# Hybrid layer: order of four engines' work around the second norm and the short filter in the mixer

## The chip, the cores and the metric

One core of one Trainium2 chip runs the whole program. The metric is the device time of one launch in microseconds (us), the median of several runs. The engines of the core are TensorE (PE; its weight loads are a row of their own, PEld), VectorE (DVE), ScalarE (ACT), GpSimd (POOL) and SyncE (SP), which issues most DMAs.

## The reference

The input x has 8 sequences of 2048 tokens with 256 channels. Four residual layers follow each other, each on a layer norm of x:

```
x = x + scan_mixer(norm(x))       # in_proj, selective scan over 8 heads, rmsnorm, out_proj
x = x + gated_ffn(norm(x))        # shift mix, sigmoid(r) * (relu(k)**2 @ W_v)
x = x + long_conv(norm(x))        # in_w, short filter of 3 taps, long convolution, out_w
x = x + gated_ffn(norm(x))
...
h = alpha * h + beta * Bx_prev + gamma * Bx_t     # one step of the scan, state 64 x 128 per head
y_t = einsum("bhpn,bhn->bhp", h, C_t)
```

The keys B and C of the scan are rotated by an angle that accumulates over the tokens. The short filter is a causal convolution of 3 taps on each of 768 channels.

## The kernel before, in words

The program has five stages one behind the other. Two short ones normalise the tokens and work out the scan's parameters and the filter's taps. The third, `mixer_and_first_ffn`, is the longest; it runs from about 240 us to about 3500 us. The fourth is the long convolution, the fifth the projection and the second gated layer. The change touches the third alone.

**Tiles and quads.** A tile is 128 tokens, so there are 128 tiles; four consecutive tiles are a quad, so there are 32 quads. The scan, the rotation and the output projection work on one tile at a time. The gated layer, the second norm and the first product of the third layer (`widen`) work on a whole quad.

**Rounds.** The body of every engine is written out by hand. `rounds(body)` runs 34 rounds; each has four places q = 0 to 3. In a place, `tile(q, lag, step)` issues a step for the tile that is `lag` tiles behind the current one, and `quad(lag, step)` issues a step for the quad that is `lag` rounds behind. An engine executes its steps strictly in the written order. Steps of different engines are tied by one semaphore per kind of step: `wait_for(engine, step, i)` waits until step number i is done.

**The steps of a tile.** TensorE makes the products of C and B for two groups of four heads (`project_bc`, L721), VectorE rotates them into two halves (`rotate`, L1159 and L1160), GpSimd adds the halves (`add_turned`, L1059), TensorE turns the sum over (`turn_over`, L744) and ScalarE copies it out of the bank (`copy_turned`, L924). GpSimd makes `masked_steps` (L1050), TensorE sums them to the decay's logs (`decay_logs`, L729 and L730), ScalarE takes their exponentials (`exponentials`, L908) and the bounds of the diagonal (`own_bounds`, L915), VectorE cuts the one by the other (`cut_decay`, L1173). One tile later TensorE makes the product `gram` (L754), VectorE weighs it with the decay (`weigh_gram`, L1179), TensorE forms the `outputs` (L769, L772), and VectorE takes them (`take_y`, L1187 and L1189). `new_state` (L780), `fade_state` (L1071) and `carry_state` (L1194) hand the state on. `decay_values` (L1065) and `gate_values` (L1167) weigh the values. A tile later still the squares are made (`square_y`, L929), paired (`pair_sums`, L1077) and summed (`sum_over`, L787), and the result is projected (`project_out`, L793) and added to x (`residual1`, L1212).

**The steps of a quad that the change moves or passes.** `residual2` (L1237, with the statistics at L1199, L1202 and L1205) adds the gated layer to x, in two halves. `layer_rstd` (L1091 to L1094) makes scale and shift on GpSimd, `normalised` (L940) the normalised tokens on ScalarE, both in two halves. `x2n_over` (L833) turns them over on TensorE; it waits for both halves. `x2_hi` (L969) and `x2_lo` (L1243) split the turned values into two parts, and six times `widen` (L840) multiplies them with the weights, one block of 128 channels at a time. `take_up` (L979, L980) takes a block out of the bank with the first tap, `taps` (L1248) adds the other two taps out of the same bank, and `before_filter` (L1110 to L1118) makes the two columns that reach over the quad's edge.

**Banks.** The eight banks of PSUM are shared by fixed rotas. All gram products and the values share one bank: the second `gram` of a tile waits for the first `weigh_gram`. The logs and the new state share another: the second `decay_logs` of a tile waits for `carry_state`. Two banks carry everything behind the scan, in the order of `BANK_POST`; in bank 1 `sum_over` of q = 2 comes after the fifth `widen` (numbered from 0) and therefore waits for `taps` 5, and the second half of `x2n_over` comes after the output projection of q = 0 and waits for `residual1`.

```
BANK_GRAM = (("gram0", "mix0", 1, -1), ("gram1", "mix1", 1, -1), ("values", "gate_values", 1, 0))
BANK_ARG = (("logs0", "exp0", 1, 0), ("new_state", "carry_state", 1, -1), ("logs1", "exp1", 1, 0))
Y_BANK, OUT_BANK, W_BANK = (1, 0, 1, 1), (1, 0, 1, 1), (1, 0, 1, 1, 0, 1)
```

Of the kernel before, what the change touches and what calls it, by code (L numbers as in the profile page):

```python
# [524 lines left out]
def mixer_and_first_ffn(nc, ctx, t):  # L525
# [116 lines left out]
    with nc.Block() as block:  # L642
# [69 lines left out]
        def _(pe):  # L712
# [131 lines left out]
            def body(tile, quad, n):  # L844
                for q in range(QUAD):
                    tile(q, 0, project_bc, 0, 1)
                    tile(q, 0, project_bc, 0, 0)
                    if q == 2:
                        quad(2, widen, 5)
# [35 lines left out]
                    if q == 0:  # L885
                        quad(2, x2n_over)
# [4 lines left out]
                    tile(q, 0, decay_logs, 1)  # L891
            rounds(body)

        @block.scalar
        def _(act):
# [88 lines left out]
            def body(tile, quad, n):  # L984
                for q in range(QUAD):
                    tile(q, -1, split_xnT)
                    tile(q, 1, exponentials, 1)
                    tile(q, 2, square_y)
                    tile(q, 0, own_bounds, 0)
                    if q == 1:  # L990
                        quad(2, x2_hi, 0)
                        quad(2, x2_hi, 1)
                    if q == 2:
                        quad(2, take_up, 5)
                    if q == 3:
                        quad(1, tanh, 0)
                    tile(q, 1, copy_turned, 1, 1)
                    tile(q, 1, copy_turned, 1, 0)
                    tile(q, 2, mean_square, q)
                    if q == 0:  # L1000
                        quad(2, normalised, 2, 0)
                    if q == 1:
                        quad(2, take_up, 0)
                    if q == 2:
                        quad(1, earlier_token, 0)
                        quad(1, earlier_token, 1)
                    if q == 3:
                        quad(1, tanh, 1)
                    tile(q, 0, exponentials, 0)
                    tile(q, 0, own_bounds, 1)  # L1010
                    if q == 0:
                        quad(2, normalised, 2, 1)
                    if q == 1:
                        quad(2, take_up, 1)
                        quad(2, take_up, 2)
                    tile(q, 0, copy_turned, 0, 1)
                    if q == 1:
                        quad(2, take_up, 3)
                    if q == 2:
                        quad(1, relu_squared, 0)  # L1020
                    tile(q, 0, copy_turned, 0, 0)
                    if q == 1:
                        quad(1, normalised, 1, 0)
                        quad(1, normalised, 1, 1)
                        quad(2, take_up, 4)
                    if q == 2:
                        quad(1, relu_squared, 1)
# [3 lines left out]
        def _(pool):  # L1031
# [90 lines left out]
            def body(tile, quad, n):  # L1122
                for q in range(QUAD):
# [6 lines left out]
                    tile(q, 1, fade_state)  # L1130
                    if q == 0:
                        quad(2, layer_rstd, 2, 0)
                        quad(2, before_filter)
                    tile(q, 2, scan_rstd)
                    tile(q, 0, add_turned, 1, 1)
                    tile(q, 0, masked_steps, 1)
                    if q == 0:
                        quad(2, layer_rstd, 2, 1)
                    tile(q, 0, add_turned, 1, 0)
# [8 lines left out]
        def _(dve):  # L1148
# [114 lines left out]
            def body(tile, quad, n):  # L1263
                for q in range(QUAD):
                    tile(q, 0, rotate, 0, 1)
                    tile(q, 1, cut_decay, 1)
                    tile(q, 0, rotate, 0, 0)
                    if q == 0:
                        quad(2, residual2, 0)
# [3 lines left out]
                    if q == 2:  # L1273
                        quad(2, taps, 4)
                    tile(q, 1, weigh_gram, 0)
                    if q == 2:
                        quad(2, taps, 5)
                    tile(q, 0, rotate, 1, 1)
                    tile(q, 1, weigh_gram, 1)
                    if q == 0:  # L1280
                        quad(2, residual2, 1)
# [10 lines left out]
                    tile(q, 0, rotate, 1, 0)  # L1292
                    if q == 1:
# [564 lines left out]
```

How the kernel before makes its waits and increments, by code:

```python
def wait(eng, sem, value):  # L34
    if isinstance(value, int) and value <= 0:
        return
    eng.wait_ge(sem, value)
# [47 lines left out]
        @block.sync  # L86
        def _(sp):
            sp.wait_ge(consts, 1)
            sp.dma_start(w_scal[:, :, 0:24], t["w_scal"].rearrange("(k p) n -> p k n", p=128)).then_inc(w_in, 16)
            def load(n, g, v):
                wait(sp, xn_ready, n - R + 1)
                sp.dma_start(xg[v % R][:, :, :], t["x"][bass.ds(n * 4 * TOK, 4 * TOK), :]
                             .rearrange("(q p) c -> p q c", p=128)).then_inc(x_in[v % R], 16)
            rounds(sp, lambda on: on(0, load))
# [74 lines left out]
        @block.tensor  # L170
        def _(pe):
            pe.wait_ge(consts, 2)
            pe.wait_ge(w_in, 16)
            def transpose(n, g, v):
# [31 lines left out]
        @block.scalar  # L207
# [13 lines left out]
                p = v % 2  # L221
                wait(act, rows_ready, n + 1)
                wait(act, scal_ready, n - 1)
                nc.scalar.copy(scT[p][:, :], p_scT[p][:, :]).then_inc(rows_taken, 1)
            def body(on):
                on(1, copy_and_store)
                on(2, take_rows)
            rounds(act, body)
            for p in range(2):
                act.wait_ge(xt_out[p], 16 * GROUPS // 2)
# [40 lines left out]
        @block.sync  # L272
# [16 lines left out]
            for k in range(KT):  # L289
                sp.dma_start(taps[:, k, TOK - 1:], t["decay"][k * 128:(k + 1) * 128, :]).then_inc(s["weights_in"], 16)
            sp.wait_ge(s["scan_dve"], PARAMS)
            sp.dma_start(t["params_dram"], params[:, :, :]).then_inc(s["stored"], 16)
```

## Time and profile before

| what | value |
|---|---|
| median of 3 runs | 4691.2 us (4690.49 to 4694.54) |
| the profiled execution | 4688.05 us |
| its span | 4686.3 us |
| TensorE busy | 4287.6 us (91%) |
| VectorE busy | 3240.8 us (69%) |
| GpSimd busy | 2370.2 us (51%) |
| ScalarE busy | 2158.3 us (46%) |
| mean granted clock of TensorE | 0.959 |

A time of "start, length" is counted from the start of the span. Consecutive operations of one engine overlap a little in the records, so the distance of two starts is often some 0.1 us less than the length shown. "idle before" is the time in which the engine had nothing to run just before an instruction, and the name behind the arrow is what the records show as ending it; "issue" means that the profile shows nothing for it, although the engine may have stood at a semaphore. The granted clock is a share of TensorE's full clock: 1.00 stands for 2.4 GHz, 0.50 for 1.2 GHz.

### The profile page before, as it was taken

To read this page: it belongs to the slowest core of one execution; us is meant where nothing else is said; L and a number is where in the kernel's file an instruction comes from. 1 tells how busy PE (TensorE), PEld (TensorE's weight loads), DVE (VectorE), ACT (ScalarE), POOL (GpSimd) and SP (SyncE) were. 2 spreads that over 40 slices of the span, in tenths; PEclk is the share of its full clock that TensorE was granted. 3 is DMA by queue.
4 is the path that set the end of the run, shared out by engine and by line. 5 is a ranking of instruction groups with operands and counts; after the bars stand their busy time and mean duration, and the time that the engine had idled before them with its cause. 6 is when DMAs were issued, how large, how long until landed. Compare 5 with 4: busy or idle time off the path is not lost. (4 is left out here: it accounts for less than half of the span.)

```text
span 4686.3 us, 118726 instructions
## 1 busy us (share of the span) xinstructions
PE 4287.6 (91%) x39924; PEld 3567.5 (76%) x39924; DVE 3240.8 (69%) x6737; ACT 2158.3 (46%) x5046; POOL 2370.2 (51%) x3284
## 2 busy tenths in 40 slices
PE   5399999999999999999999999999959999989999
PEld 3177777777777777777777777777738888878888
DVE  8766666666677666667666676666645666658888
ACT  3244444444444444444444444444426666645555
POOL 3275666665666665666565666565610000016666
PEclk9699999999999999999999999999979999999999
DMA  8311111111111111111111111111127666633333
GB/s 274 134 50 36 35 37 42 40 37 43 37 37 46 36 37 46 34 37 48 36 35 46 34 38 48 35 37 43 32 53 191 183 183 181 183 110 106 105 105 95
DMA packets 369775, 347.50 MB, mean 74 GB/s; under 512 B 24954, under 2 KB 343290, under 8 KB 360186
## 3 DMA queue, kind: packets, MB, share of 16 engines
q1 hardware_dynamic: 352380, 323.98, 23.3%
q10 hardware_dynamic: 16896, 16.78, 1.1%
q8 instruction: 324, 5.31, 0.5%
q14 instruction: 175, 1.43, 0.1%
HBM read 232.01 MB, written 108.66 MB: 73 GB/s over the span
## 5 line engine op out<-in xcount | busy, mean ns | idle before, releaser
L721 PE MATMUL bank<-w_bc,xnT 128*128 128x512 f32 x3072 | 814.7, 408 | 10.7 <-POOL xnT L1042 10.7
L924 ACT COPY turned_t<-bank 128x512 f32<-128x512 f32 x512 | 299.9, 586 | 857.5 <-PE bank L744 857.4
L721 PEld LDWEIGHTS bank<-w_bc,xnT 128*128 128x128 f32 x3072 | 569.5, 192 | 149.9 <-issue 35.3
L1050 POOL TENSOR_TENSOR steps<-upto,par 128x512 fp32r<-128x512 f32 x512 | 551.0, 1097 | 6.2 <-PE bank L730 6.2
L1455 PE MATMUL p_yc<-sig,toep 64*64 64x256 f32 (+14 forms) x16384 | 539.6, 282 | 15.2 <-issue 11.9
L1455 PEld LDWEIGHTS p_yc<-sig,toep 64*64 64x64 f32 x16384 | 476.0, 132 | 91.0 <-issue 44.5
L1159 DVE TENSOR_TENSOR rot<-bank,par 128x512 f32<-128x512 f32 x512 | 350.0, 684 | 247.1 <-PE bank L721 165.5
L1059 POOL TENSOR_TENSOR turned_b<-rot 128x512 f32<-128x512 f32 x256 | 325.3, 1271 | 306.5 <-DVE rot L1160 306.1
L754 PEld LDWEIGHTS bank<-turned_t 128*128 128x128 f32 x2048 | 300.7, 214 | 127.8 <-issue 105.3
L754 PE MATMUL bank<-turned_t 128*128 128x128 f32 x2048 | 309.5, 300 | 93.9 <-issue 92.3
L1179 DVE TENSOR_TENSOR mix<-bank,decay 128x512 f32<-128x512 f32 x256 | 175.6, 686 | 298.5 <-PE bank L754 297.9
L1042 POOL TENSOR_TENSOR xnT<-xnT_raw,xnT 128x256 fp32r<-128x256 f32 x128 | 94.8, 741 | 504.0 <-ACT xnT L903 504.0
L1604 POOL MEMSET xT<- 128x258 f32 x1 | 0.3, 314 | 686.7 <-POOLq L1349 686.7
L1160 DVE TENSOR_TENSOR rot<-bank,par 128x512 f32<-128x512 f32 x512 | 347.1, 678 | 0.0
L840 PE MATMUL bank<-x2T,in_w 128*128 128x512 f32 x1152 | 315.8, 411 | 26.6 <-ACT ms_eps L934 17.0
L1059 POOL TENSOR_TENSOR turned_c<-rot 128x512 f32<-128x512 f32 x256 | 332.4, 1299 | 1.9 <-DVE rot L1160 1.8
L915 ACT ACTIVATE own<-bound,par 128x128 f32<-128x128 f32 x1024 | 326.4, 399 | 0.4 <-DMA par<-params_dram 0.4
L1248 DVE SCALAR_TENSOR_TENSOR conv<-bank,short,conv 128x511 f32<-128x511 f32 (+1 forms) x384 | 286.1, 745 | 47.6 <-ACT conv L980 30.9
L840 PEld LDWEIGHTS bank<-x2T,in_w 128*128 128x128 f32 x1152 | 215.0, 191 | 77.8 <-DVE x2T L1243 20.4
L1487 DVE TENSOR_TENSOR ys<-p_yc,odd_y 64x256 f32<-64x256 f32 x256 | 95.6, 411 | 238.7 <-ACT odd_y L1406 238.7
L780 PEld LDWEIGHTS bank<-u_w,turned_b 128*128 128x128 f32 x2048 | 250.5, 193 | 10.8 <-issue 0.3
L940 ACT ACTIVATE xn<-x_quad,shift,rstd 128x256 f32<-128x256 f32 x256 | 136.5, 593 | 264.2 <-POOL shift L1094 264.2
(264 smaller groups left out, 9727.3 us busy)
## 6 DMA issues: line engine op xcount, KB each, us to landing
toep<-taps_dram SPq DMA_DIRECT2D x256, 260.0 KB, 4.2
el<-el_dram SPq DMA_DIRECT2D x256, 128.0 KB, 3.1
xg<-arg_x SPq DMA_DIRECT2D x32, 512.0 KB, 4.9
xnT_dram<-xt_g ACTq DMA_DIRECT2D x32, 512.0 KB, 4.2
xnT_raw<-xnT_dram SPq DMA_DIRECT2D x128, 128.0 KB, 2.5
x_quad<-arg_x SPq DMA_DIRECT2D x32, 512.0 KB, 3.9
x_dram<-x_quad SPq DMA_DIRECT2D x32, 512.0 KB, 3.8
x0T_dram<-conv SPq DMA_DIRECT2D x32, 512.0 KB, 2.8
```

The lines of the kernel that those rows point to most:

```text
L721: last = mm(p_bc[c][:, :], xnT[w.q % 2][p][:, k, :], w_bc[q][:, k, c * 1024 + g * W4:c * 1024 + (g + 1) * W4], start=(n == 0), stop=(n == ...
L754: last = mm(p_gram[:, c], turned_t[g][0][:, c], turned_t[g][1][:, c], start=True, stop=True)
L780: last = mm(p_state[:, v], turned(w, h // GROUP, 0)[:, (h % GROUP) * STATE:(h % GROUP + 1) * STATE], u_w[:, v], start=True, stop=True)
L840: last = mm(p_post[W_BANK[e]][:, :], in_w[q][:, k, e * 128:(e + 1) * 128], x2T[p][:, k, :], start=(m == 0), stop=(m == len(SPLIT) - 1))
L915: last = s_.activation(own[g][:, h * TOK:(h + 1) * TOK], bound[:, :], ACT.Identity, scale=par[w.p][:, w.q, P_RHO + g * GROUP + h:P_RHO + g ...
L924: s_.copy(turned_t[g][c][:, :], p_tr[:, :]).then_inc(s[f"copy_{BC[c]}"], 1)
L1050: last = g_.tensor_tensor(heads(steps[p][:, :]), upto[:, :].unsqueeze(1).broadcast_to([128, GROUP, TOK]), over(of_group(P_A + p * HEADS, w ...
L1059: g_.tensor_tensor(turned(w, g, c)[:, :], rot1[c][:, :], rot2[c][:, :], ALU.add).then_inc(s[f"turn_{BC[c]}"], 1)
L1159: v_.tensor_tensor(heads(rot1[c][:, :]), heads(p_bc[c][:, :]), cos, ALU.mult)
L1160: v_.tensor_tensor(parts(rot2[c][:, :]), parts(p_bc[c][:, :])[:, :, ::-1, :], over(sin.rearrange("p (h s) -> p h s", s=2), STATE // 2), AL ...
L1248: last = v_.scalar_tensor_tensor(out=conv[:, e, back:], in0=p_post[W_BANK[e]][:, 0:SPAN - back], scalar=short[:, e, 2 - back:3 - back], in ...
L1455: last = mm(by_seq(p_y[p][c][odd * H:(odd + 1) * H, 0:2 * TILES])[:, :, first:], toep[n % SLOTS][c * H:(c + 1) * H, lag * H:(lag + 1) * H] ...
```

## The change

Steps change their places within the body of four engines; none is added, removed or altered.

- TensorE: `widen` 5 leaves q = 2 for the end of q = 1; in q = 0 `x2n_over` comes behind the second `decay_logs` instead of ahead of it.
- ScalarE: in q = 1 and 2 `x2_hi` and `take_up` 5 come ahead of `square_y` and the first `own_bounds`; in q = 0 the two halves of `normalised` each come behind a `copy_turned` (the first was ahead of the exponentials).
- GpSimd, q = 0: the second `masked_steps` comes ahead of the `add_turned` of group 1; the halves of `layer_rstd` come behind one `add_turned` each, and `before_filter` behind all.
- VectorE: in q = 0 the halves of `residual2` come behind the second weighing and behind the last rotation, where they were ahead of the first weighing and behind the second; in q = 1 `x2_lo` comes ahead of `cut_decay` and the second rotation; in q = 2 `taps` 4 comes ahead of the first rotation and `taps` 5 behind it.

```diff
@@ tensor @@
-                    if q == 2:
-                        quad(2, widen, 5)
                     if q == 3:
                         quad(1, receptance, 0)
                     tile(q, 1, gram, 0)
...
                     tile(q, 0, project_u)
-                    if q == 0:
-                        quad(2, x2n_over)
                     if q == 1:
                         quad(2, widen, 4)
                     if q == 2:
                         quad(1, key, 1)
                     tile(q, 0, decay_logs, 1)
+                    if q == 0:
+                        quad(2, x2n_over)
+                    if q == 1:
+                        quad(2, widen, 5)
@@ scalar @@
                     tile(q, 1, exponentials, 1)
-                    tile(q, 2, square_y)
-                    tile(q, 0, own_bounds, 0)
                     if q == 1:
                         quad(2, x2_hi, 0)
                         quad(2, x2_hi, 1)
                     if q == 2:
                         quad(2, take_up, 5)
+                    tile(q, 2, square_y)
+                    tile(q, 0, own_bounds, 0)
...
                     tile(q, 2, mean_square, q)
-                    if q == 0:
-                        quad(2, normalised, 2, 0)
...
                     tile(q, 0, own_bounds, 1)
-                    if q == 0:
-                        quad(2, normalised, 2, 1)
...
                     tile(q, 0, copy_turned, 0, 1)
+                    if q == 0:
+                        quad(2, normalised, 2, 0)
...
                     tile(q, 0, copy_turned, 0, 0)
+                    if q == 0:
+                        quad(2, normalised, 2, 1)
@@ gpsimd @@
                     tile(q, 1, fade_state)
+                    tile(q, 2, scan_rstd)
+                    tile(q, 0, masked_steps, 1)
+                    tile(q, 0, add_turned, 1, 1)
                     if q == 0:
                         quad(2, layer_rstd, 2, 0)
-                        quad(2, before_filter)
-                    tile(q, 2, scan_rstd)
-                    tile(q, 0, add_turned, 1, 1)
-                    tile(q, 0, masked_steps, 1)
+                    tile(q, 0, add_turned, 1, 0)
                     if q == 0:
                         quad(2, layer_rstd, 2, 1)
-                    tile(q, 0, add_turned, 1, 0)
+                        quad(2, before_filter)
@@ vector @@
+                    if q == 2:
+                        quad(2, taps, 4)
                     tile(q, 0, rotate, 0, 1)
-                    tile(q, 1, cut_decay, 1)
-                    tile(q, 0, rotate, 0, 0)
-                    if q == 0:
-                        quad(2, residual2, 0)
                     if q == 1:
                         quad(2, x2_lo, 0)
                         quad(2, x2_lo, 1)
                     if q == 2:
-                        quad(2, taps, 4)
+                        quad(2, taps, 5)
+                    tile(q, 1, cut_decay, 1)
+                    tile(q, 0, rotate, 0, 0)
                     tile(q, 1, weigh_gram, 0)
-                    if q == 2:
-                        quad(2, taps, 5)
                     tile(q, 0, rotate, 1, 1)
                     tile(q, 1, weigh_gram, 1)
                     if q == 0:
-                        quad(2, residual2, 1)
+                        quad(2, residual2, 0)
...
                     tile(q, 0, rotate, 1, 0)
+                    if q == 0:
+                        quad(2, residual2, 1)
```

## Rows read from the trace of the kernel before

**Rows 1.** The page: shares of the span, and the granted clock in 40 slices.
```profile
PE 4287.6 (91%) x39924; PEld 3567.5 (76%) x39924; DVE 3240.8 (69%) x6737; ACT 2158.3 (46%) x5046; POOL 2370.2 (51%) x3284
...
PEclk9699999999999999999999999999979999999999
```

**Rows 2.** Windows: busy time per engine (PE, PEld, DVE, ACT, POOL), then granted clock.
```profile
500.00:3100.00 2600.00, 2450.05 (x15261) 2030.93 (x15261) 1782.34 (x3161) 1139.18 (x2649) 1603.13 (x1971) 0.97 0.13 40
...
1602.00:1608.00 6.00, 5.73 (x28) 4.86 (x29) 4.15 (x10) 2.74 (x7) 5.43 (x14) 0.50 0.01 4
...
1550.00:1554.00 4.00, 2.76 (x20) 2.43 (x20) 1.28 (x3) 2.13 (x7) 4.00 (x5) 1.00 0.00 0
...
1652.00:1656.00 4.00, 3.80 (x17) 3.41 (x18) 0.00 (x0) 3.38 (x10) 3.60 (x5) 0.57 0.02 4
```

**Rows 3.** Waits of PE from 500 to 3100 us: total, times, longest.
```profile
PE bank L754 <- issue: 76.9, 25, 3.3
PE bank L787 <- DVE conv L1248: 41.8, 26, 1.9
PE bank L840 <- ACT ms_eps L934: 14.5, 26, 0.7
```

**Rows 4.** Timeline of PE in one q = 0: start, length, line, shapes, count.
```profile
1594.97 1.06 PE L754 MATMUL bank<-turned_t 128*128 128x128 f32 x8
1595.86 0.60 PE L744 MATMUL bank<-ident,turned_c 128*128 128x128 f32 x4
...
1602.27 2.04 PE L754 MATMUL bank<-turned_t 128*128 128x128 f32 x8 [3.28 <-issue]
...
1615.48 1.03 PE L833 MATMUL bank<-ident,xn 128*128 128x128 f32 x8
1616.27 0.47 PE L729 MATMUL bank<-steps,after_r 128*128 128x512 f32 x1
...
1616.81 0.39 PE L721 MATMUL bank<-w_bc,xnT 128*128 128x512 f32 x1
```

**Rows 5.** Timeline of DVE in the same q = 0.
```profile
1595.04 1.43 DVE L1173 TENSOR_TENSOR decay<-decay,own 128x512 f32<-128x512 f32 x1
...
1597.84 1.31 DVE L1237 SCALAR_TENSOR_TENSOR x_quad<-gate,x_quad 128x512 f32<-128x512 f32 x1 [0.17 <-issue]
...
1601.21 0.68 DVE L1179 TENSOR_TENSOR mix<-bank,decay 128x512 f32<-128x512 f32 x1
1601.81 0.67 DVE L1159 TENSOR_TENSOR rot<-bank,par 128x512 f32<-128x512 f32 x1
...
1605.20 0.69 DVE L1237 SCALAR_TENSOR_TENSOR x_quad<-gate,x_quad 128x512 f32<-128x512 f32 x1 [0.16 <-issue]
...
1607.97 0.41 DVE L1187 TENSOR_TENSOR y_from<-bank,el 128x256 f32<-128x256 f32 x1
...
1608.82 0.69 DVE L1159 TENSOR_TENSOR rot<-bank,par 128x512 f32<-128x512 f32 x1
...
1614.93 0.68 DVE L1173 TENSOR_TENSOR decay<-decay,own 128x512 f32<-128x512 f32 x1
```

**Rows 6.** Timelines of three engines around the change from q = 1 to q = 2.
```profile
1541.34 0.77 ACT L980 ACTIVATE conv<-bank,all_taps_b,short 128x512 f32<-128x512 f32 x1
...
1548.53 1.56 DVE L1248 SCALAR_TENSOR_TENSOR conv<-bank,short,conv 128x511 f32<-128x511 f32 x2
...
1550.83 0.35 PE L787 MATMUL bank<-ones,y_sum 128*128 128x1 f32 x2 [1.90 <-DVE conv L1248]
```

**Rows 7.** Timelines of POOL and ACT in the q = 0 of rows 4.
```profile
1597.34 1.27 POOL L1059 TENSOR_TENSOR turned_c<-rot 128x512 f32<-128x512 f32 x1
...
1608.99 0.70 POOL L1091 TENSOR_TENSOR rstd<-var_eps,minus_half 128x2 f32<-128x2 f32 x1
...
1610.00 0.20 POOL L1094 TENSOR_TENSOR shift<-minus_mean,rstd 128x2 f32<-128x2 f32 x1
...
1610.23 1.09 ACT L940 ACTIVATE xn<-x_quad,shift,rstd 128x256 f32<-128x256 f32 x2 [4.00 <-POOL shift L1094]
```

## The prediction

> **What bounds the kernel now.** I read four views in this order: shares and clock slices of the page, the waits of PE over 26 steady rounds of the mixer, one round's engines in order of time, and the windows of granted clock. PE is busy 91% of the span, and its clock is below full in only a few slices [rows 1]. In the mixer, from 500 to 3100 us, PE works 2450 of 2600 us at a mean granted clock of 0.97 [rows 2]. So PE is the bound there, and what can be won is its idle time and the work that it does at half clock.
>
> The idle time has three places that come back in every round of four tiles [rows 3]: the second gram product (L754), 76.9 us in 25 waits, 3.08 each; the sum over the squares (L787), 41.8 us in 26 waits, 1.61 each; the first widening product (L840), 14.5 us in 26, 0.56 each. Together 5.25 us a round. The clock adds its own loss: 3% of 2600 us at half the full rate are 0.03 x 2 x 2600 = 156 us at half clock, which lose 78 us of work, 3.0 us a round. So 8.25 us a round is the ceiling for anything that only reorders, and a round is some 100 us.
>
> The first place is q = 0. PE ends the first decay logs at 1602.27 - 3.28 = 1598.99 and stands for 3.28 us [rows 4]. What it waits for is the gram bank, freed by the weighing (L1179), which runs at 1601.21 to 1601.89 because the first residual2 block stands ahead of it from 1597.84 [rows 5]. After the wait the window 1602 to 1608 has a granted clock of 0.50 [rows 2], the lower of the two levels, 1.2 GHz, and L754 x8 takes 2.04 us where it took 1.06 before the wait [rows 4]. The second place is q = 2: PE stands 1.90 us at L787 until the last taps (L1248, from 1548.53) have read the bank [rows 6]. In a later round of the same kind the clock falls there too: 0.57 over 1652 to 1656 [rows 2].
>
> **The change part by part.** No instruction is added or removed; each one is moved within its own engine's order. No DMA is moved. SP's waits stay (the store of x2 waits for residual2, as before), so its queue is passed by nothing.
>
> *Residual2 behind the weighing (VectorE, q = 0).* The block costs 1601.21 - 1597.84 = 3.37 us in the first place and 1607.97 - 1605.20 = 2.77 in the second [rows 5]; I take 3.1, and keep both ends. It now follows the second weighing, and its other half follows the last rotation. I go through this round again in the new order, with its own durations. Rotations and cut decay end at about 1597.84 - 0.17 = 1597.67, as before. The first weighing starts at once and takes 0.60 start to start (1601.21 to 1601.81) [rows 5]: done at 1598.3, 0.7 us before PE reaches gram 1 at 1598.99. That wait is gone, by this sum, with a margin of 0.7 us. The rotation of group 1 must wait for GpSimd's turned copy, 1597.34 + 1.27 = 1598.6 [rows 7], and takes 1.2 (two operations at 0.60 start to start): to 1599.9. Gram 1 takes 0.89 (1594.97 to 1595.86) [rows 4] and ends at 1599.9, the second weighing at 1600.6. Then residual2 0 (0.17 of drain and 3.1): 1603.9. take_y 0 takes 1608.82 - 1607.97 = 0.85 [rows 5]: 1604.8. Rotation of group 1, other side, 1.2: 1606.0. residual2 1 with its drain, 3.3: 1609.3. GpSimd's rstd to shift takes 1610.00 + 0.20 - 1608.99 = 1.2 [rows 7], ScalarE's norm 1.09 [rows 7]; with some 0.1 us at each handover x2n_over can start at 1612.0.
>
> *Turned copies ahead of the norm (ScalarE) and masked steps behind the first logs (GpSimd).* The exponentials of group 0 no longer wait behind a norm, and GpSimd's second masked steps come before add_turned and the rstd. They fill time in which both engines waited; I cost them at nothing. Their cover is the 4 us that ScalarE waited for the shift before each norm [rows 7]. If it is gone, the delay of the norm falls straight on PE, as below.
>
> *x2n_over behind the second logs (PE, q = 0).* From gram 1 (1602.27) to the next tile (1616.81) PE needs 14.54 us, of which some 5.8 at half clock count half: 11.6 at full clock, 0.79 of it x2n_over (1615.48 to 1616.27) [rows 4]. Unhindered PE would reach x2n_over at 1598.99 + 10.8 = 1609.8. It is not let in before 1612.0. So **2.2 us of waiting come back** where 3.28 went: about 0.5 ahead of the second logs, which need carry_state and with it the end of residual2 1 on VectorE, the rest ahead of x2n_over. Bounds from the two lengths of the block: 1.6 to 2.8 us. Whether the clock falls in the new waits no row can say. From below: not at all, 0. From above: as much as now, 3.0 us a round. The nearest rows are those behind the q = 2 wait (clock at 1.00 over 1550 to 1554 in the one round, 0.57 over 1652 to 1656 in the other) [rows 2], so I take a part of it, 0.85 us a round, half a stretch such as 1652 to 1656 in every round.
>
> *Filter's fifth widening and taps (PE, VectorE, q = 1 and 2).* The fifth product leaves q = 2 and comes at the end of q = 1: the same work on PE. Its taps are then run behind the first rotation instead of behind the weighing, about 5 us before the sum over the squares instead of 1.9 us after it was due, so all 1.61 goes. Taps 4 now stand ahead of the first rotation: their input is taken up by 1541.34 + 0.77 = 1542.1 [rows 6], they end near 1543.7, and the rotation, whose products end 1.4 us later than before, was due near 1544.4. Margin 0.7 us. Cost nothing.
>
> *x2_lo ahead of cut_decay and a rotation (VectorE, q = 1).* The first widening waits for it 0.56 us now. x2_lo ends by the new order before PE is due at widen 0: 0.56 gained. The weighing behind it is late by the same 1.3 us, which still ends about 1 us before gram 1.
>
> **Sum.** Now lost: 3.08 + 1.61 + 0.56 + 3.0 = 8.25 us a round. Left: 2.2 + 0.85 = 3.05. Gain 5.2 us in each of 31 rounds (of 34, those in which all three lags have a quad): 161 us. The profiled execution took 4688.05 us (span 4686.3), 3.1 below the median of 4691.2. 4688 - 161 = 4527, against the median 4530.
>
> **A rule against the change.** The cut decay that runs beside GpSimd's masked steps took 1.43 us, and without them 0.68 [rows 5]. The Trainium skill, "SBUF — State Buffer", "Who interferes with whom", says that a DVE instruction with two SBUF inputs and a GpSimd instruction that reads SBUF exclude each other for a whole instruction, and that order of issue decides who waits. This trace agrees, by the two lengths just named. As a mechanism here: the first operation of each residual2 block has both inputs in SBUF, and the new places put it beside the masked steps and the added turned copies. Each could wait out one more GpSimd operation of 1.0 to 1.3 us, which makes the rival "port" below.
>
> **The rivals.**
> - *The clock falls as before.* The new waits stand close together, 2.2 us within some 3, and the old 3.28 dropped the clock in each round. For: the q = 2 wait of under 2 us did so at times. Against: at times it did not. Left 2.2 + 3.0: gain 3.05 x 31 = 95, time 4596. Chance 0.22.
> - *Port.* Both blocks 1 us longer, wait 4.2, clock lost as before: left 7.2, gain 1.05 x 31 = 33, time 4658. Against: the lengths that I took already hold one such collision (3.37). Chance 0.07.
> - *Better.* The norm is in time to within 1.2 us and the clock stays up: gain 7.05 x 31 = 219, time 4472. Chance 0.09.
> - *Slower.* x2n_over stands in PE's queue ahead of the next tile's products, and x2_lo in VectorE's ahead of the next rotation and the weighing. Every us by which the second norm is late beyond the reckoned 1612.0 is then lost whole. With the clock as before it costs more than the change gains once the wait passes 8.25 - 3.0 = 5.25 us, that is 3 us later than reckoned. Two us more for each block would give a wait of 6.2: 0.95 x 31 = 29 us more, 4720. For: the chain residual2 1, rstd, norm, turn has no slack at all in the new order. Against: its operations have lengths known to 0.6 us. Chance 0.04.
> - *No effect.* The weighing was not what PE waited for, or VectorE becomes the bound over the whole round. VectorE is busy 1782 of 2600 us [rows 2], so only a stretch of it can bind. Time 4690. Chance 0.03.
>
> **How the numbers follow.** My forecast (both waits gone, 2.2 back, clock lost in part) has the remaining 0.55 and reaches from 4485 to 4565. With the clock rival the range is 4482 to 4602, which leaves out the port, the slower case, no effect and part of the better one. A measurement of this kernel can tell about 0.2% (9 us) from no change. Faster by more than that: 0.55 + 0.22 + 0.07 + 0.08, 0.92 in all; within it 0.03; slower 0.05.
>
> **What would show it.** In the changed profile: no wait at L754 with the half clock behind it; L787's wait at L1248 gone; a new wait of PE, 1.5 to 2 us, at L833 for ScalarE's norm, and a short one at L729 or L730; the round near 95 us; clock about 0.99 over the mixer. I am wrong if L754 still waits, if the wait at L833 is over 3 us, or if the granted clock of the mixer is still 0.97.

## The result and the profile after

The changed kernel takes 4491.7 us (median of 4 runs, 4485.8 to 4495.2) against 4690.8 for the kernel before; the ratio is 0.9575, with a 95% interval from 0.9563 to 0.9587. That is 199 us less where 161 were forecast. The profiled execution took 4485.8 us, its span is 4484.1. The number of instructions is the same.

The page of the changed kernel, shares of the span and the granted clock in 40 slices, as in [rows 1]:

```profile
PE 4197.9 (94%) x39924; PEld 3488.0 (78%) x39924; DVE 3222.6 (72%) x6737; ACT 2157.4 (48%) x5046; POOL 2376.0 (53%) x3284
...
PEclk9699999999999999999999999999979999999999
```

PE's busy time fell by 90 us although it does the same work. The clock accounts for it: a mean of 0.959 over 4686.3 us lacks 192 us of full clock, one of 0.978 over 4484.1 us lacks 99, which is 93 less. The window of the mixer shows the same (time, then busy time of PE, PEld, DVE, ACT, POOL, then the granted clock), as in [rows 2]:

```profile
500.00:2900.00 2400.00, 2345.81 (x15012) 1937.76 (x15012) 1745.14 (x3116) 1122.91 (x2613) 1584.99 (x1934) 1.00 0.13 42
```

The clock is 1.00 where it was 0.97: in this stretch it never stands at half, where before it did so for 143 us. PE works 2346 of 2400 us. The waits of PE in the same stretch (total, times, longest), as in [rows 3]:

```profile
PE bank L833 <- ACT xn L940: 20.8, 25, 0.9
PE bank L801 <- issue: 20.0, 52, 0.6
PE bank L840 <- issue: 6.7, 26, 0.4
PE bank L833 <- issue: 2.0, 9, 0.3
```

The waits at L754 and L787 are gone. New is 0.83 us at L833, the turn of the second norm. L801, the turn of the first norm, takes 0.77 us a round in two parts. The stores of x2, one a round, start at 408.0 us first and 3267.7 last, 2859.7 / 31 = 92.2 us apart in the mean; before it was (3466.1 - 412.1) / 31 = 98.5. The last two distances are short ones at the end of the stage (84.4 and 51.1 us now). A full round takes 94.0 us, and took 100.4 (the table in the next section).

One q = 0 on PE, to be held against [rows 4] (start, length, line, shapes, count, idle time before):

```profile
1520.03 0.39 PE L730 MATMUL bank<-steps,after_r 128*128 128x512 f32 x1
1520.40 1.16 PE L754 MATMUL bank<-turned_t 128*128 128x128 f32 x8
...
1531.15 0.40 PE L730 MATMUL bank<-steps,after_r 128*128 128x512 f32 x1
1532.38 1.37 PE L833 MATMUL bank<-ident,xn 128*128 128x128 f32 x8 [0.83 <-ACT xn L940]
1533.50 3.03 PE L721 MATMUL bank<-w_bc,xnT 128*128 128x512 f32 x12
```

Gram 1 follows the logs at once and runs at full clock, 1.16 us instead of 2.04. The same stretch on VectorE, against [rows 5]:

```profile
1519.03 0.68 DVE L1179 TENSOR_TENSOR mix<-bank,decay 128x512 f32<-128x512 f32 x1
...
1522.45 1.37 DVE L1237 SCALAR_TENSOR_TENSOR x_quad<-gate,x_quad 128x512 f32<-128x512 f32 x1 [0.17 <-issue]
...
1525.05 0.22 DVE L1205 TENSOR_SCALAR var_eps<-mean_var 128x2 f32<-128x2 f32 x1
1525.25 0.42 DVE L1187 TENSOR_TENSOR y_from<-bank,el 128x256 f32<-128x256 f32 x1
...
1527.53 0.69 DVE L1237 SCALAR_TENSOR_TENSOR x_quad<-gate,x_quad 128x512 f32<-128x512 f32 x1 [0.16 <-issue]
...
1529.45 0.45 DVE L1205 TENSOR_SCALAR var_eps<-mean_var 128x2 f32<-128x2 f32 x1
1529.81 0.68 DVE L1194 TENSOR_TENSOR state<-bank,state 128x512 f32<-128x512 f32 x1
```

The weighing ends at 1519.71, 0.7 us before gram 1 starts. The two blocks of residual2 take 1525.25 - 1522.45 = 2.80 and 1529.81 - 1527.53 = 2.28 us.

### The profile page after: what moved, and what is told of

The parts are those of the page before. It is cut to its first block and busy times, and to the rows that moved or that the text cites. A ratio compares the mean times of both kernels' runs of the same rounds, so it can differ in the third digit from the quotient of the medians.

```text
span 4484.1 us, 118726 instructions
## 1 busy us (share of the span) xinstructions
PE 4197.9 (94%) x39924; PEld 3488.0 (78%) x39924; DVE 3222.6 (72%) x6737; ACT 2157.4 (48%) x5046; POOL 2376.0 (53%) x3284
## 5 line engine op out<-in xcount | busy, mean ns | idle before, releaser
L721 PE MATMUL bank<-w_bc,xnT 128*128 128x512 f32 x3072 | 804.3, 404 | 11.7 <-POOL xnT L1042 11.7
L721 PEld LDWEIGHTS bank<-w_bc,xnT 128*128 128x128 f32 x3072 | 556.8, 189 | 144.7 <-issue 34.5
L1050 POOL TENSOR_TENSOR steps<-upto,par 128x512 fp32r<-128x512 f32 x512 | 536.6, 1068 | 0.0
L1059 POOL TENSOR_TENSOR turned_c<-rot 128x512 f32<-128x512 f32 x256 | 354.5, 1385 | 1.8 <-DVE rot L1160 1.8
L840 PE MATMUL bank<-x2T,in_w 128*128 128x512 f32 x1152 | 315.4, 410 | 18.7 <-issue 9.0
L1042 POOL TENSOR_TENSOR xnT<-xnT_raw,xnT 128x256 fp32r<-128x256 f32 x128 | 108.8, 850 | 384.2 <-ACT xnT L903 384.2
L754 PEld LDWEIGHTS bank<-turned_t 128*128 128x128 f32 x2048 | 265.3, 191 | 31.8 <-ACT turned_t L924 13.0
L754 PE MATMUL bank<-turned_t 128*128 128x128 f32 x2048 | 273.5, 276 | 0.7 <-DVE u_g L1167 0.4
L840 PEld LDWEIGHTS bank<-x2T,in_w 128*128 128x128 f32 x1152 | 214.9, 191 | 69.6 <-issue 21.4
L780 PEld LDWEIGHTS bank<-u_w,turned_b 128*128 128x128 f32 x2048 | 248.5, 192 | 10.3 <-issue 0.2
L1091 POOL TENSOR_TENSOR rstd<-var_eps,minus_half 128x2 f32<-128x2 f32 x128 | 90.7, 708 | 294.8 <-DVE var_eps L1205 291.7
```

The source lines that it names most:

```text
L721: last = mm(p_bc[c][:, :], xnT[w.q % 2][p][:, k, :], w_bc[q][:, k, c * 1024 + g * W4:c * 1024 + (g + 1) * W4], start=(n == 0), stop=(n == ...
L754: last = mm(p_gram[:, c], turned_t[g][0][:, c], turned_t[g][1][:, c], start=True, stop=True)
L780: last = mm(p_state[:, v], turned(w, h // GROUP, 0)[:, (h % GROUP) * STATE:(h % GROUP + 1) * STATE], u_w[:, v], start=True, stop=True)
L840: last = mm(p_post[W_BANK[e]][:, :], in_w[q][:, k, e * 128:(e + 1) * 128], x2T[p][:, k, :], start=(m == 0), stop=(m == len(SPLIT) - 1))
L1050: last = g_.tensor_tensor(heads(steps[p][:, :]), upto[:, :].unsqueeze(1).broadcast_to([128, GROUP, TOK]), over(of_group(P_A + p * HEADS, w ...
L1059: g_.tensor_tensor(turned(w, g, c)[:, :], rot1[c][:, :], rot2[c][:, :], ALU.add).then_inc(s[f"turn_{BC[c]}"], 1)
```

## The experiments

All medians below stand against a kernel before of 4690.8 to 4695.0 us, run beside them on the same chip. The gains in us of different groups of runs can therefore be off by some 4 us against each other.

One table for all of them: the mean of 26 full rounds, from the second store of x2 to the 28th. A round is PE's busy time and its idle time. The work of PE is the same in all, 588 matmuls a round, so what differs in the busy time is how long the work took. "Half clock" is the time in which the granted clock stood at 0.50; some of it falls where PE is idle and costs nothing.

| kernel | round, us | PE busy | PE idle | half clock |
|---|---|---|---|---|
| before | 100.4 | 94.5 | 5.9 | 6.2 |
| changed | 94.0 | 91.8 | 2.1 | 0 |
| 1 `res_group` | 96.5 | 92.7 | 3.8 | 1.2 |
| 2 `filter_group` | 99.0 | 94.4 | 4.6 | 6.8 |
| 3 `split_group` | 100.7 | 95.3 | 5.4 | 8.5 |
| 4 `res_alone` | 103.3 | 96.4 | 6.8 | 10.6 |
| 5 `undo_residual` | 98.3 | 94.0 | 4.3 | 5.4 |
| 6 `fill_wait` | 100.2 | 93.0 | 7.2 | 2.4 |
| 7 `late_norm_3` | 94.9 | 92.3 | 2.6 | 0.4 |
| 8 `late_norm_8` | 98.0 | 94.0 | 4.1 | 4.8 |
| 9 `partners_only` | 101.0 | 95.1 | 5.9 | 7.5 |
| 10 `partners_fill` | 99.0 | 93.7 | 5.3 | 3.4 |
| 11 `over_later` | 92.6 | 91.5 | 1.1 | 0 |
| 12 `over_and_sum` | 91.8 | 91.3 | 0.5 | 0 |

**1. The q = 0 part alone** (`res_group`). The kernel before with the moves of residual2 and its partners, and none of the filter's.

```diff
-  q 0, VectorE: rotate, residual2 0, weigh 0, rotate, weigh 1, residual2 1, take_y 0, rotate
+  q 0, VectorE: rotate, weigh 0, rotate, weigh 1, residual2 0, take_y 0, rotate, residual2 1
+  and: norms, layer_rstd, before_filter, masked_steps, x2n_over as in the change
```

> The kernel before with the q = 0 part of the change alone (residual2, both norms, rstd, masked steps, turn of the second norm); the filter's steps stay where they were. Theory (the weighing freed the gram bank late, and the idle time also halved the clock): PE's 3.08 us wait at L754 and the half clock behind it go, about 0.8 us come back at L833. 3.08 + 2.35 - 0.8 = 4.6 us in 31 rounds, 143 us: about 4548 us. Rival (the clock costs nothing of its own, because VectorE bounds q = 0): only 3.08 - 0.8 = 2.3 us a round, about 4620 us.

Measured: 4566.8 us, ratio 0.9744 (0.9728 to 0.976), 124 us gained. That is nearer to the theory's 143 than to the rival's 70. PE's waits from 500 to 2900 us:

```profile
PE bank L787 <- DVE conv L1248: 41.1, 25, 2.1
PE bank L833 <- ACT xn L940: 21.2, 25, 0.9
```

The wait at L754 is gone, 0.85 us came back at L833, as forecast for this run. The mean granted clock of the mixer is 0.99, and the work of PE takes 1.8 us a round less. So the half clock did have a price of its own, against the rival.

**2. The filter's part alone** (`filter_group`).

```diff
-  q 2: widen 5 | take_up 5 behind own_bounds | taps 4, taps 5 around the first weighing
+  q 1, end: widen 5 | q 2: take_up 5 ahead of square_y | taps 4, rotate, taps 5
```

> The kernel before with the filter's part alone: the fifth widening at the end of q = 1, taps 4 and 5 and their take-ups earlier. Theory: the wait of 1.61 us at L787 and the half clock that sometimes follows it (0.65 us a round) go, some 0.4 us come back at the next turn (L801): 1.9 us in 31 rounds, 58 us, about 4633 us. Rival (the wait only moves on to the next step of the same bank, the turn of the first norm behind the mean square): under 10 us gained, 4682 us or more.

Measured: 4642.6 us, ratio 0.9898 (0.9881 to 0.9914), 48 us gained. The wait at L787 is gone, and more stands at L801 than before, 0.74 us a round instead of about 0.4:

```profile
PE bank L754 <- issue: 73.8, 24, 3.3
PE bank L801 <- issue: 17.8, 48, 0.6
```

The rival falls, and the theory holds for the waits. Its clock term, 0.65 us a round, did not come: the mean of the mixer is still 0.97, PE's busy time is that of the kernel before, and the half clock now stands behind the wait at L754 alone.

**3. x2_hi and x2_lo alone** (`split_group`).

```diff
-  q 1: square_y, own_bounds, x2_hi | rotate, cut_decay, rotate, x2_lo, weigh
+  q 1: x2_hi, square_y, own_bounds | rotate, x2_lo, cut_decay, rotate, weigh
```

> The kernel before with x2_hi and x2_lo earlier in q = 1 and nothing else. Theory: PE's wait of 0.56 us at the first widening shrinks to the 0.26 us seen after the whole change: 0.3 us in 31 rounds, 9 us, about 4681 us. Rival (what is gained at the widening is lost at gram 1, whose weighing now comes 1.3 us later): no difference, 4690 us.

Measured: 4691.1 us, ratio 0.9997 (0.9987 to 1.0007): nothing. The waits and the window of 500 to 2900 us, one fence for each:

```profile
PE bank L754 <- issue: 70.7, 23, 3.2
PE bank L787 <- DVE conv L1248: 39.1, 24, 2.0
...
PE bank L840 <- issue: 6.4, 24, 0.4
```

```profile
500.00:2900.00 2400.00, 2273.44 (x14026) 1888.50 (x14024) 1633.97 (x2905) 1046.38 (x2436) 1476.82 (x1811) 0.96 0.12 39
```

The wait at L840 did shrink, from 0.56 to 0.27 us, and nothing new stands at gram 1, so the rival's reason is not what took it. What took it is the clock. Over the span it is 0.952 to 0.954 in all ten executions, against 0.956 to 0.960 in those of the kernel before. By the table PE idles 0.5 us a round less and needs 0.8 us more for the same work. The half clock is new in q = 2: the wait at L787, as long as before, is followed by it in all 24 rounds of the window, and was in 9 of 24 before. Why the earlier x2_lo brings this is open.

**4. residual2 without its partners** (`res_alone`). VectorE as in run 1; ScalarE, GpSimd and PE as before.

> The kernel before with only the two halves of residual2 moved on VectorE; ScalarE, GpSimd and PE keep their old order. Theory (the partners are needed): ScalarE's exponentials and GpSimd's add_turned and masked steps now stand behind a norm that comes some 6 us later, so the new state, the second logs or the turn of the second norm make PE wait; of the 143 us that the group is to bring under half is left: 4620 to 4690 us. Rival (the partners only fill idle time, and residual2 is all of it): as the group, about 4550 us.

Measured: 4771.9 us, ratio 1.0177 (1.016 to 1.0194): **81 us slower than before, 205 us slower than with the partners**, beyond the range of the theory too. The timeline of PE in one q = 0:

```profile
1531.75 1.65 PE L721 MATMUL bank<-w_bc,xnT 128*128 128x512 f32 x6
1537.46 3.65 PE L780 MATMUL bank<-u_w,turned_b 128*128 128x64 f32 x16 [4.07 <-issue]
1540.90 1.06 PE L744 MATMUL bank<-ident,turned_c 128*128 128x128 f32 x4
1541.76 3.62 PE L793 MATMUL bank<-w_out,yT 128*128 128x256 f32 x8
```

And that of ScalarE:

```profile
1535.79 1.09 ACT L940 ACTIVATE xn<-x_quad,shift,rstd 128x256 f32<-128x256 f32 x2 [6.05 <-POOL shift L1094]
1536.79 0.57 ACT L908 ACTIVATE decay<-bank 128x512 f32<-128x512 f32 x1
```

ScalarE stands 6.05 us in its queue at the norm, which now comes late. The exponentials behind it free the bank that the new state needs (`BANK_ARG`); they end at 1537.36, and PE goes on at 1537.46. It stands 4.07 us at L780 instead of 3.28 at L754. Behind the wait the new state takes 3.65 and the output projection 3.62 us, where both took 1.9 us in the kernel before: the granted clock is 0.50 from 1537.5 to 1545. By the table the idle time grew by 0.95 us a round and the busy time by 1.95.

**5. The changed kernel with residual2 put back** (`undo_residual`).

> The changed kernel with only the halves of residual2 put back on VectorE (ahead of the first weighing and behind the second). Theory: the 3.1 us wait at L754 and its half clock come back in 31 rounds and the 0.8 us at L833 go, 4.6 us a round: 4634 us. The partners then gain nothing by themselves; what is left is what the filter's part brought alone (48 us measured). Rival (partners bring part of the gain without residual2, since ScalarE's exponentials no longer wait behind a norm): 4600 us or less.

Measured: 4616.6 us, ratio 0.9838 (0.9821 to 0.9854). PE's wait at L754 is back with 73.5 us in 24 waits. The time lies between the theory's 4634 and the rival's 4600. This kernel differs from run 2 by the partners and by x2_hi and x2_lo, and these seem to bring 26 us. Run 9 tests whether the partners do so by themselves.

**6. PE's wait filled** (`fill_wait`). The kernel before; in q = 0 one projection, whose operands are ready, goes ahead of gram 1.

```diff
+  if q == 0:
+      tile(q, 0, project_bc, 1, 0)
   tile(q, 1, gram, 1)
...
-  tile(q, 0, project_bc, 1, 0)
+  if q != 0:
+      tile(q, 0, project_bc, 1, 0)
```

> The kernel before, with one projection of q = 0 (six matmuls, 1.5 us) moved ahead of gram 1, into PE's 3.28 us wait; VectorE's order as before. Theory (the idle time halves the clock, and that costs 2.3 to 3.0 us a round of its own): the idle time shrinks to 1.8 us, the clock stays up in most rounds, and the gain is 1.5 + about 2: 3.5 x 31 = 108 us, 4583 us. Rival (the half clock is free, since VectorE bounds q = 0 anyway): 1.5 us a round or less, 4645 us or more.

Measured: 4688.2 us (4677 to 4706), ratio 0.9995 (0.9981 to 1.001). **Nothing, so my theory fell here.** The clock of the mixer did go up, to 0.99, and no wait at L754 is followed by half clock any more (before: every one); in 2 of 24 rounds it falls later in q = 0. The waits from 500 to 2900 us (lines from L721 on stand 3 lower than in the kernel before, so L927 is the copy of the turned values):

```profile
PE bank L744 <- ACT turned_t L927: 44.7, 24, 2.0
PE bank L787 <- DVE conv L1251: 39.3, 24, 2.1
PE bank L754 <- issue: 38.7, 23, 1.7
PE bank L780 <- issue: 21.6, 24, 0.9
```

One q = 0 on ScalarE shows what L744 waits for:

```profile
1503.36 1.09 ACT L943 ACTIVATE xn<-x_quad,shift,rstd 128x256 f32<-128x256 f32 x2 [4.13 <-POOL shift L1097]
1504.36 0.56 ACT L927 COPY turned_t<-bank 128x512 f32<-128x512 f32 x1
```

The wait at L754 fell from 3.1 to 1.7 us. 1.9 us came at L744 and 0.9 at L780, where there was none. Both are steps of ScalarE queued behind a norm, and the norm waits for residual2 on VectorE. So q = 0 of the kernel before had a second limit right behind the visible one: VectorE's two blocks, GpSimd's rstd, ScalarE's norm, ScalarE's copy, PE's turn. By the table PE's work takes 1.5 us a round less and its waits are 1.3 us longer: what the clock gives back ends up in the waits on that chain. The rival was right that filling gains nothing; its reason (VectorE) is the head of the chain only. Run 10 tests this reading.

**7. and 8. The norm made late** (`late_norm_3`, `late_norm_8`). The changed kernel with 3 or 8 more statistics in the second half of residual2, whose results are not used; the edit is that of the first.

```diff
   dve.drain()
+  if h == 1:
+      for e in range(3):
+          v_.bn_stats(spare[:, e, :], x[pp][:, 2, :])
   moments(2, [2 * h, 2 * h + 1], x[pp], "residual2")
```

> The changed kernel with three more statistics operations (their results are not used) inside the second half of residual2, some 1.2 us, so that PE's wait ahead of the second norm's turn is about the 2.2 us that the prediction reckoned. Theory A (the norm's chain has no slack, the clock holds): 1.2 us a round, 37 us more than the changed kernel: 4529 us, granted clock of the mixer 1.00. Theory B (a wait of 2 us drops the clock at times, as priced at 0.85 us a round): 2.05 us a round, 64 us: 4555 us, mean granted clock of the mixer 0.99 or less.

> The same with eight more statistics operations, some 3.3 us, a wait of about 4.1 us. Theory (idle time of this length halves the clock in every round, at 2.3 to 3.0 us on top): 3.3 + 2.6 = 5.9 us a round, 183 us: 4675 us, granted clock of the mixer 0.97. Rival (no clock loss): 3.3 x 31 = 102 us, 4594 us.

Measured: 4521.1 us (ratio to the kernel before 0.9639, 0.9623 to 0.9655) and 4622.5 us (0.9854, 0.9837 to 0.987), so 29 and 131 us more than the changed kernel. The waits of the first (lines one lower: L730 is the first product of the second logs, L834 the turn of the norm):

```profile
PE bank L834 <- ACT xn L941: 23.2, 26, 0.9
...
PE bank L730 <- DVE state L1195: 11.9, 25, 1.3
```

And of the second:

```profile
PE bank L730 <- DVE state L1195: 52.4, 25, 2.4
PE bank L834 <- ACT xn L941: 20.6, 25, 0.9
```

With three, PE waits 0.46 + 0.89 = 1.4 us a round and the window still has a clock of 1.00. That is theory A, but not quite: the clock did fall to half in 3 of the 26 rounds. The time grew by 29 / 31 = 0.9 us a round, 0.5 of it idle time and 0.4 slower work. With eight PE waits 2.10 + 0.82 = 2.9, and the window reads

```profile
500.00:2900.00 2400.00, 2298.77 (x14375) 1892.58 (x14373) 1732.12 (x3187) 1077.49 (x2507) 1525.22 (x1866) 0.98 0.13 40
```

By the table the idle time grew by 1.9 us a round and the busy time by 2.1. Together 4.1, and measured are 131 / 31 = 4.2. So the time lies between theory (5.9) and rival (3.3 without a clock loss). **Here PE is the bound, and the half clock costs its full price**, about as much again as the wait that sets it off. The added operations took less than I had reckoned: they start 0.33 us apart, so eight delay the norm by some 2.7 us and not 3.3, three by 1.0 and not 1.2. They showed as 2.1 and 0.46 us at PE, since carry_state had 0.44 us of slack ahead of the second logs (1530.93 - 1530.49 in the changed kernel). A wait of 2.2 us a round, as the prediction had it, was not reached by either.

**9. The partners alone** (`partners_only`) and **10. the partners with the wait filled** (`partners_fill`). Both are the kernel before with ScalarE's, GpSimd's and PE's moves of q = 0 and residual2 in its old place; run 10 adds the edit of run 6.

> The kernel before with only the partners of residual2 moved (both norms behind the turned copies on ScalarE, rstd and before_filter behind add_turned and the masked steps on GpSimd, the turn of the second norm behind the second logs on PE); residual2 itself stays ahead of the first weighing. Theory (in the kernel before, ScalarE's queue with the norms in it is a second limit of q = 0; taking it away alone leaves the 3.1 us wait at L754): the same 26 us that lie between the filter's part alone (4643) and the changed kernel with residual2 put back (4617): 4665 us. Rival (the partners only pay together with a residual2 that comes later): 4690 us.

> The kernel before with those partners moved and, as in the run that filled the wait, one projection of q = 0 ahead of gram 1. Theory (there the new waits at the new state, 0.90 us, and at turned_b, 1.86 us, were ScalarE's norms and gave everything back): without the norms in the way the filled 1.5 us and the kept clock of some 1.5 us count: 3 us in 31 rounds below the partners alone, about 4575 us, PE's waits at L780 and L744 gone. Rival (VectorE itself, with both halves of residual2 early, bounds q = 0): within 20 us of the partners alone, 4645 us or more, with a new wait behind an operation of VectorE.

Measured: 4699.9 us (ratio 1.0019, 1.001 to 1.0029) and 4647.3 us (0.9902, 0.9887 to 0.9918). The partners alone gain nothing; they lose 0.2%. Nor do x2_hi and x2_lo alone (run 3). The 26 us between runs 5 and 2 are therefore a matter of the company: with the filter's part done they are there, without it they aren't. The table places them, 0.3 us a round of idle time (L840) and 0.4 of slower work. Which of the two moves brings the latter was not tried. Filling the wait, worth nothing in run 6, is now worth 53 us, or 1.7 us a round. That is below the theory's 3 us and above the rival's 20 us in all. The waits of run 10 (lines lower by 3, as in run 6):

```profile
PE bank L754 <- issue: 40.6, 24, 1.7
PE bank L787 <- DVE conv L1251: 39.2, 24, 1.9
PE bank L833 <- ACT xn L943: 20.5, 25, 1.1
```

L744 and L780 are gone from the list, as the theory had it, and 0.8 us came up at the turn of the norm, which I had left out of the sum. The clock is 0.98: no wait at L754 is followed by half clock, but each of the 24 at L787 is.

**11. and 12. Taking away what is left** (`over_later`, `over_and_sum`).

```diff
   tile(q, 0, project_bc, 0, 1)
+  if q == 1:
+      quad(2, x2n_over)
   tile(q, 0, project_bc, 0, 0)
...
   tile(q, 0, decay_logs, 1)
-  if q == 0:
-      quad(2, x2n_over)
```

Run 12 has besides, in q = 2, `sum_over` ahead of the second `turn_over` of group 1 on PE and `mean_square` ahead of the second `copy_turned` on ScalarE.

> The changed kernel with the turn of the second norm moved from the end of q = 0 to q = 1, between the first two projections (six matmuls, 1.4 us later). Theory (the 0.80 us wait at L833 is a pure wait for the norm, and nothing behind the turn is tight): the wait goes, 0.8 x 31 = 25 us: 4467 us. Rival (the second projection and with it gram 0 come later by the turn's 1.1 us, x2_hi and x2_lo come later too, and the first widening waits instead): no difference, 4492 us.

> The same, and in q = 2 the sum over the squares ahead of the turn of B (PE) with the mean square ahead of the copy of B (ScalarE). Theory (the 0.77 us at L801, in two parts, is mostly the turn of the first norm waiting for the mean square, which stands behind a copy): some 0.5 us a round less, 16 us: 4451 us. Rival (the copy and with it gram 1 or the bank of the turns come later by as much): no difference to the run before, 4467 us.

Measured: 4451.9 us (ratio 0.9488, 0.9475 to 0.9501) and **4426.0 us (0.9435, 0.9422 to 0.9448)**, so 40 and 66 us below the changed kernel. Both theories hold, and each brought some 10 to 15 us more than I gave it. One part of that can be named: behind the wait the turn took 1533.50 - 1532.38 = 1.12 us to the next product, against 0.79 in [rows 4] and in run 11. The waits of run 12 and its window:

```profile
PE bank L840 <- issue: 6.8, 27, 0.4
PE bank L801 <- issue: 1.7, 8, 0.3
```

```profile
500.00:2900.00 2400.00, 2386.96 (x15380) 1985.39 (x15379) 1773.67 (x3191) 1146.19 (x2671) 1631.95 (x1989) 1.00 0.14 44
```

PE now works 2387 of 2400 us at full clock. The order alone can win at most the 0.5 us a round in which PE is still idle.

## Why the prediction was right, and where it was wrong

**The direction and the place were right.** The three waits of [rows 3] were the right rows to start from. In the changed kernel two are gone and the third is halved, and the new wait is where the text put it: at the turn of the second norm, for ScalarE. The short wait that it expected at the second logs did not come.

**The number was in the range, and partly by luck.** What happened in q = 0 is what the rival "better" described: the norm in time to within 1.2 us and the clock up. That rival had a chance of 0.09 and a time of 4472, 20 us from the 4491.7 measured; the forecast's 4530 is 38 us away. Two losses that the sum put at nothing hold the time above 4472: 0.26 us a round is left at L840, and L801 waits 0.4 us longer. They took back 0.6 us a round of the 1.4 + 0.85 by which the terms of the next paragraph were too dear. A full round gained 6.4 us where 5.2 were forecast: 3.76 of idle time and 2.65 of work done faster.

**The term that was mis-sized is what comes back in q = 0**: "2.2 us of waiting come back" and 0.85 us for the clock. Measured are 0.83 us and a clock of 1.00. The wait was too long by 1.4 us for two reasons that can be read in the rows above. The blocks of residual2 take 2.80 and 2.28 us start to start, not 3.1 each, which is 1.1 us. In the first the difference is its last operation, var_eps, which took 0.92 us in the old place and takes 0.22 in the new (the last section has the rows and the reason). I took the lengths of the old places for the new ones. And PE gets through its logs 0.3 us later than I had it: at 1531.5, 17.9 us behind the start of the tile (L721 at 1513.62), where the prediction has 1609.8 against 1592.2, 17.6 us. The 0.5 us ahead of the second logs never came, since carry_state ends at 1530.49 and they start at 1530.93. For the clock, run 7 shows that with waits of 1.4 us a round it falls in 3 of 26 rounds, and run 8 that with 2.9 us it falls in 24 of 25. Whether 0.85 us is fair at the 2.2 us that I reckoned, no run shows.

**The filter's step was right in its place and wrong in a margin.** Taps 5 was said to run about 5 us before the sum over the squares. It ends at 1564.4, 1.5 us before. The prediction's own rows would have given about this: a rotation from 1544.4 on takes 1.2 us, taps 5 another 1.5, to 1547.1, and the sum over the squares was due at 1550.83 - 1.90 = 1548.9. The changed kernel:

```profile
1559.30 1.57 DVE L1248 SCALAR_TENSOR_TENSOR conv<-bank,short,conv 128x511 f32<-128x511 f32 x2 [0.74 <-ACT conv L980]
...
1561.65 0.69 DVE L1159 TENSOR_TENSOR rot<-bank,par 128x512 f32<-128x512 f32 x1 [0.78 <-PE bank L721]
...
1562.86 1.56 DVE L1248 SCALAR_TENSOR_TENSOR conv<-bank,short,conv 128x511 f32<-128x511 f32 x2
```

(VectorE of the changed kernel, q = 2.) The margin of taps 4 before the rotation was given as 0.7 us and is 0.78. What I left out is that L801 waits longer, 0.77 instead of 0.4 us, because the sum over the squares no longer holds PE ahead of it.

**x2_lo** was priced at 0.56 us, the whole wait; 0.3 us of it went, and by itself it gave no time (run 3). The weighing behind it ends at 1540.67, well ahead of gram 1 at 1542.12, as the text said.

**The partners were costed at nothing, and this is right only as an addition.** By the text they "fill time in which both engines waited". Run 4 shows what they are: without them the same move of residual2 is a loss of 81 us. The cover that I named, ScalarE's 4 us of idle time before each norm, was not free time. It was a closed queue, with the exponentials and a turned copy standing in it behind the norm. None of my rivals had this.

**The accounting of 8.25 us a round was a ceiling, not a sum of what each edit gives.** The parts alone bring 124, 48 and 0 us, together 172; the whole brings 199. In the table the idle time adds up (3.9 us a round less in the three parts, 3.8 in the whole), and the work does not: 1.75, 0.06 and -0.84 us a round less in the parts, 2.65 in the whole. Each part leaves a wait that half clock follows at times; the whole leaves none. Run 6 shows the strongest form of this: removing 1.4 us of the wait at L754 and the half clock behind it gave nothing, because another chain ended at the same time. The waits of the kernel before named the step that came last; they did not say how close the next one was. The forecast held since the change removed both at once.

**The rule on the shared port** spoke for longer blocks. One such meeting is in the new order too (L1237 takes 1.37 us in the first block, beside fade_state, and 0.69 in the second), but in sum the new places were better than the old, since var_eps met less of GpSimd's operations there. The rival built on it, 4658 us, did not come.

One slip of arithmetic: the list of chances gives 0.09 to "better" and 0.04 to "slower", the total takes 0.08 and 0.05.

## What to carry to other kernels

A wait at an engine in a strict queue is the last of several chains; before a move is priced, follow each queue that the moved step feeds and ask which steps of other work stand behind its consumer there. When a producer moves later, its consumers in the other queues must move too, or the idle time ahead of them turns into a stop for everything behind them: here that was the difference between 4772 and 4567 us. What an edit is worth alone may be nothing or a loss, so measure the group.

## What the runs showed of the hardware that was not expected

A wait of TensorE can cost twice its length. When the waits of a round went from 0.8 to 2.9 us (run 8), the mixer's mean clock fell to 0.98 and the round grew by 4.2 us; at 1.4 us (run 7) it fell in 3 of 26 rounds. The length of one wait alone does not decide it. The wait at L787 is 1.53 us in most rounds of every kernel that has it, and how often half clock follows within 9 us differs widely (500 to 2900 us):

| waits of PE | kernel | followed by half clock |
|---|---|---|
| L787, 1.5 to 2.1 us | `res_group` | 8 of 25 |
| | before | 9 of 24 |
| | `partners_only` | 14 of 24 |
| | `fill_wait` | 16 of 24 |
| | `res_alone` | 19 of 23 |
| | `split_group`, `partners_fill` | 24 of 24 each |
| L754, 2.9 to 3.3 us | before, `filter_group`, `split_group`, `undo_residual`, `partners_only` | all, 117 |
| L754, 1.5 to 1.8 us | `fill_wait`, `partners_fill` | none of 47 |
| L833, 0.8 to 1.0 us | changed, `res_group` | none of 50 |

So a reorder can change the price of a wait that it leaves as long as it was, as in run 3.

The smallest operation of VectorE in the chain, 2 values for each partition, took 0.92 us in the old place and 0.22 in the new. It ends when an operation of GpSimd ends. The kernel before, where GpSimd adds a turned copy until 1601.28 and var_eps ends at 1601.30:

```profile
1600.02 1.26 POOL L1059 TENSOR_TENSOR turned_b<-rot 128x512 f32<-128x512 f32 x1
1600.38 0.92 DVE L1205 TENSOR_SCALAR var_eps<-mean_var 128x2 f32<-128x2 f32 x1
```

And run 4, where GpSimd does nothing at that time but wait for it:

```profile
1534.29 0.17 DVE L1205 TENSOR_SCALAR var_eps<-mean_var 128x2 f32<-128x2 f32 x1
1534.54 0.71 POOL L1091 TENSOR_TENSOR rstd<-var_eps,minus_half 128x2 f32<-128x2 f32 x1 [2.02 <-DVE var_eps L1205]
```

From 500 to 2900 us all 47 such operations of the kernel before and all 50 of the changed one end 0.02 to 0.03 us after an operation of GpSimd, and take between 0.21 and 0.96 us; the 24 at this place in run 4 take 0.17. So its length is what is left of the GpSimd operation that it meets. In a chain without slack such an operation is worth a look. The Trainium skill, "SBUF — State Buffer", "Who interferes with whom", lists tensor_scalar among the operations that can take the pair of ports shared with GpSimd, when their operands meet certain conditions. These rows fit that; that it is the port, and not something else that the two engines share, no run here shows.
